# An attention and expert block on one core: expert products and two sides of a convolution issued behind the attention product, and k copied out of its bank ahead of q

## What is computed

```python
def window_attend(xh):                       # xh: 32 of the 64 channels
    q, k, v = split(einsum('oi,bihw->bohw', qkv_w, xh), 3)
    lepe = conv3x3_depthwise(v, lepe_w)
    q, k, v, lepe = part(q), part(k), part(v), part(lepe)    # 4x4 windows, 8 heads
    attn = softmax(q * scale @ k^T + bias)
    return unpart(attn @ v + lepe)
...
for s in (0, 2):                             # plain, and rolled by 2 rows and columns
    results.append(concat([window_attend(half) for half in halves(roll(ln_c(x), -s))]))
x = x + results[0] + roll_back(results[1])
t = tokens(x)
p = softmax(ln_t(t) @ router_w + router_b); top 2 of 8, renormalised
t = t + sum_over_top2(p * (ln_t(t) @ expert_w[e] + expert_b[e]))
```

## Time and profile before

| what | value |
|---|---|
| median of 3 runs | 3418.93 us (3413.72 to 3419.05) |
| the profiled execution | 3416.38 us, span 3414.6 us |
| mean granted TensorE clock | 0.942 of full |
| PE busy | 3076.2 us (90%) |
| POOL busy | 2509.8 us (74%) |
| DVE busy | 2233.1 us (65%) |
| ACT busy | 1619.7 us (47%) |
| DMA engines | mean share of some 60%, 152 GB/s |

### The profile page before, as it was taken

The page is one execution under the profiler, slowest core; times in us unless marked ns, Lnnn a source line. Parts: engine busy times, 40 slices in busy tenths (PEclk is TensorE's granted clock), DMA queues, the critical chain, the costliest instruction groups (busy, mean ns, idle before and its releaser), DMA issues.

```text
span 3414.6 us, 201082 instructions
## 1 busy us (share of the span) xinstructions
PE 3076.2 (90%) x84772; PEld 1798.8 (53%) x84772; DVE 2233.1 (65%) x4807; ACT 1619.7 (47%) x3362; POOL 2509.8 (74%) x4998
## 2 busy tenths in 40 slices
PE   4899999989989899998999989999899999999987
PEld 2555555545555455554555545555455555555553
DVE  2566767656666666666666757666666666666666
ACT  2554545445444454444444445444454444444441
POOL 4887777767777677777777767777677777777771
PEclk7999999999999999999999999999999999999998
DMA  2456665656565565556565656666565656565656
GB/s 64 105 138 160 159 160 155 160 131 168 148 167 149 145 165 147 155 153 153 150 168 147 163 139 158 161 155 166 133 170 148 168 152 163 152 162 146 163 138 178
DMA packets 436964, 517.64 MB, mean 152 GB/s; under 512 B 116400, under 2 KB 405168, under 8 KB 435888
## 3 DMA queue, kind: packets, MB, share of 16 engines
q1 hardware_dynamic: 270128, 390.67, 42.8%
q0 software_dynamic: 165888, 113.57, 13.9%
HBM read 312.67 MB, written 77.86 MB: 114 GB/s over the span
## 4 chain that ended last, share of the span: by engine, by line
PE 81%; issue 8%; DVE 5%; ACT 4%; DMA 1%; DVEq 0%; POOL 0%; SPq 0%; ACTq 0%; POOLq 0%
PE bank L632 18%; PE bank L717 14%; PE bank L697 13%; PE bank L617 9%; PE bank L723 4%; PE bank L657 3%; PE bank L670 3%; PE bank L737 3%; PE bank L742 2%; PE bank L731 2%; PE bank L756 2%; PE bank L648 2%; PE bank L748 2%; ACT qx L820 2%; ACT bank L812 1%
## 5 line engine op out<-in xcount | busy, mean ns | idle before, releaser
L585 POOL DMA_DIRECT2D vx<-vt x3072 | 1562.1, 517 | 443.6 <-PE bank L723 433.8
L573 POOL DMA_DIRECT2D kx<-k_sb x1536 | 739.2, 489 | 386.7 <-issue 241.7
L717 PEld LDWEIGHTS bank<-probT,vx 128*32 128x32 f32 x36864 | 605.5, 150 | 445.9 <-issue 387.8
L717 PE MATMUL bank<-probT,vx 128*32 128x16 f32 x36864 | 668.0, 210 | 146.9 <-issue 132.7
L632 PEld LDWEIGHTS bank<-kx,qx 32*32 32x32 f32 x36864 | 598.1, 112 | 345.4 <-issue 332.4
L632 PE MATMUL bank<-kx,qx 32*32 32x64 f32 x36864 | 700.7, 226 | 76.6 <-issue 54.2
L949 DVE TENSOR_TENSOR gx<-gate_wide,yn_pair 128x768 f32<-128x768 f32 x384 | 365.6, 953 | 384.5 <-PE bank L617 380.4
L697 PE MATMUL bank<-halo,conv_w 128*64 128x380 f32 (+6 forms) x2592 | 479.5, 497 | 0.1
L806 ACT ACTIVATE prob<-prob 128x512 f32<-128x512 f32 x576 | 360.0, 625 | 244.4 <-DVE prob L961 222.3
L961 DVE TENSOR_TENSOR prob<-bank,row_max 128x512 f32<-128x512 f32 x576 | 398.5, 692 | 16.7
L956 DVE TENSOR_REDUCE row_max<-bank 128x32 f32<-128x512 f32 x576 | 382.8, 665 | 37.8 <-PE bank L632 33.2
(11 more groups left out here) (72 smaller groups left out, 2959.9 us busy)
## 6 DMA issues: line engine op xcount, KB each, us to landing
gate_wide<-gate_rows SPq DMA_DIRECT2D x768, 192.0 KB, 3.9
vx<-vt POOLq DMA_DIRECT2D x3072, 12.0 KB
halo<-xn SPq DMA_DIRECT2D x160, 240.0 KB
kx<-k_sb POOLq DMA_DIRECT2D x1536, 24.0 KB
z<-fin SPq DMA_DIRECT2D x192, 192.0 KB
yn_pair<-yn POOLq DMA_DIRECT2D x384, 96.0 KB, 3.2
xa<-in_x SPq DMA_DIRECT2D x96, 192.0 KB, 3.1
xn<-xa SPq DMA_DIRECT2D x192, 96.0 KB, 2.5
```

Of the source, the lines that this page charges most:

```text
L573: pool.dma_start(kx[to + m:to + C:4, r % 2, m, :], k_sb[at + m:at + C:4, r % 2, :])\
L585: pool.dma_start(vx[to:to + TOK, r % 2, col:col + 25:8, odd, :], vt[at:at + TOK, r % 2, x::2, :, :].rearrange("p h n k -> p h (n k)"))\
L717: last = MM(bank_o[32 * c:32 * c + 32, at * TOK:(at + 1) * TOK], vx[:, kr % 2, :, at % 2, at // 2 * 4 + ba], probT[:, kr % 2, at, ba * TOK ...
```

## The change

Three things move, nothing is added or taken away. On TensorE sides 1 and 2 of the convolution (slots 5 and 0), expert 2 (slot 1) and expert 3 (slot 2) are issued behind the product of their slot; expert 3 gets the key (2, 1) for that. The router and centre still follow the sides. On ScalarE k is copied ahead of the two copies of q. On VectorE y_out moves from the middle of slot 2 to its end.

```diff
-EXPERT_AT = {(0, 0): 0, (1, 0): 1, (1, 1): 2, (2, 0): 3}
+EXPERT_AT = {(0, 0): 0, (1, 0): 1, (1, 1): 2, (2, 1): 3}
...
+                def conv(sides):
+                    ti = s.in_tile("conv")
+                    if not ti or ti[2] not in sides:
+                        return
                     k, r, side = ti
                     t, dw = (r + 1) % IMT, SIDES[side]
                     if side == 0:
...
                     if side == 2:
                         last.then_inc(conv_made, 1)
+
...
-                expert(1)
...
-                if (ti := s.in_tile("conv")) and ti[2] < len(SIDES):
...
+                conv((0,))
                 if u := s.unit("product"):
                     n, r = u
                     k, kr, j = s.in_strip("product")
...
                     last.then_inc(pv_made, 1)
+                expert(1)
+                conv((1, 2))
                 if ti := s.tile("centre"):
...
                 if st := s.strip("query_key"):
+
+                    k, r = st
+                    act.wait_ge(k_made, k + 1)
+                    if s.later(r, 2):
+                        act.wait_ge(k_spread[r % 2], k // 2 * (K_DMAS * 16))
+                    S.activation(by_window(k_sb[:, r % 2, :]), windows(bank_p[1][:, 0:SPX]),
+                                 ACT.Copy).then_inc(k_saved, 1)
+                if st := s.strip("query_key"):
                     k, r = st
                     if s.later(r, 2):
                         act.wait_ge(score_made, (k - 1) * UNITS)
...
-                if st := s.strip("query_key"):
-
-                    k, r = st
-                    act.wait_ge(k_made, k + 1)
-                    if s.later(r, 2):
-                        act.wait_ge(k_spread[r % 2], k // 2 * (K_DMAS * 16))
-                    S.activation(by_window(k_sb[:, r % 2, :]), windows(bank_p[1][:, 0:SPX]),
-                                 ACT.Copy).then_inc(k_saved, 1)
...
                 gate_product(0)
-                if yt := s.tile("tile_out"):
-                    k, r = yt
-                    dve.wait_ge(expert_made, (k + 1) * PAIRS)
-                    if s.later(r, 2):
-                        dve.wait_ge(out_stored[r % 2], k // 2 * 16)
-                    V.tensor_tensor(y_out[:, r % 2, :], bank_f[:, 0:SPX], y[:, r % 4, :], ALU.add).then_inc(y_out_made, 1)
...
                 gate_work((10, 12), (0, 0))
+                if yt := s.tile("tile_out"):
+                    k, r = yt
+                    dve.wait_ge(expert_made, (k + 1) * PAIRS)
+                    if s.later(r, 2):
+                        dve.wait_ge(out_stored[r % 2], k // 2 * 16)
+                    V.tensor_tensor(y_out[:, r % 2, :], bank_f[:, 0:SPX], y[:, r % 4, :], ALU.add).then_inc(y_out_made, 1)
```

More of the change, by code:

```diff
@@ L619, in expert @@
                     last.then_inc(expert_made, 1)
+                def conv(sides):
+                    ti = s.in_tile("conv")
+                    if not ti or ti[2] not in sides:
+                        return
+                    k, r, side = ti
+                    t, dw = (r + 1) % IMT, SIDES[side]
+                    if side == 0:
+                        pe.wait_ge(halo_loaded[r % 2], halos_to(s, r) * 16)
+                        if s.later(r, 1):
+                            pe.wait_ge(y_step, k * 2 - 1)
+                    low, high = max(0, -dw), W - max(0, dw)
+                    first = [side == 0, side == 0]
+                    for group, skip in ((0, 0), (1, 2)):
+                        parts = [(half, *rows) for half in range(2) for rows in conv_rows(t, half)[group]]
+                        for half, top, end, which in sorted(parts, key=lambda part: part[1]):
+                            at = half * SP + skip
+                            last = MM(by_rows(bank_c[half * C:(half + 1) * C, 0:SPX])[:, top:end, low:high],
+                                      conv_w[:, which, group * 3 + side, :],
+                                      by_rows(halo[:, r % 2, :])[:, at + top:at + end, low + dw:high + dw],
+                                      start=first[half], stop=(side == 2 and group == 1), skip_group_check=True)
+                            first[half] = False
+                    if side == 2:
+                        last.then_inc(conv_made, 1)
                 if u := s.unit("score"):
```

## The result

The changed kernel takes 3320.29 us (median of 4 runs, 3301.59 to 3324.2) against 3416.32 us for the kernel before (4 runs, 3407.16 to 3419.05) beside it: ratio 0.972, 95% interval 0.9691 to 0.975, 96 us less. The profiled execution took 3319.92 us with a span of 3318.1, 96.5 us less than the span before.

The account below looks back on a forecast made before the run. TensorE, busy 90% of the span, was taken to bound the kernel with its waits and lowered clock. Terms -32 - 5 + 25 - 53 + 9 = -56 us took 3418.9 to 3363 us, range 3300 to 3420.

Parts of the forecast that it names:

- k ahead of q: Slot 3: k copied 0.92 us earlier on ScalarE shortens tile_sum's wait for k; -32 us, bounds 0 and -47.
- Bias: Score of slot 3: its wait for the bias goes in some 33 tiles; -5 us, bounds 0 and -18.
- Clock: TensorE behind slot 3's standstill: clock falls less often, 31 stretches of 1.71 us fewer; -53 us, at most 164.
- as about half the tiles keep gaps of near 2 us in sum: Step in sizing the clock gain: the reason to take only a third of the possible 164 us, giving -53 us.
- rival of the clock staying up: No standstill above 1 us in slot 3, so 137 us of clock return: sum -140, 3279 us; chance 0.13.
- 116 stretches: Low-clock stretches of TensorE over the span before the change, 198 us lost in all, more than one to a tile.
- Code blocks: Code-load gaps in slots 2 to 4 and 0: -35, +45 and +15 at most; together +25 us, bounds -35 and +60.
- 3.87 us from restart to restart: TensorE, product of slot 3 to score of slot 4: time between restarts after code gaps, taken to stay.
- The product of slot 5: Without side 1 as cover it waits 0.1 to 0.2 us for fin of the strip before; +9 us.
- Code loading takes it all back: Rival: loads of slots 2 to 4 set the pace, k's gain reappears as gaps; about -15 us, 3404; chance 0.17.
- Code loading doesn't care for the order: Rival: a gap is as long wherever the block ends, code term nought; sum -81, 3338 us; chance 0.08.
- Slower, by loads 2 us later: Rival: SP's loads, 2 us later, fall on the code load slot 4 waits for; 3440 us; chance 0.12.

Follow-up runs that it names:

- e4: The changed kernel with side 1 alone put back ahead of the product of slot 5, side 2 left behind that of slot 0: 3292.23 us, ratio 0.9682.
- e3: The changed kernel with all three sides of the convolution ahead of the product again; experts, y_out and k stay moved: 3280.94 us, ratio 0.965.
- e1: The kernel before with one edit, k alone copied ahead of q: 3370.12 us, ratio 0.9915 to the kernel before.
- e10: The kernel before with only experts 2 and 3 behind the product and y_out at the slot's end: 3360.97 us, ratio 0.989.
- e8: The changed kernel with gate rows spread over 16 of 384 columns, so part of the computation is left out: 3196.75 us, ratio 0.9401.

## Why the prediction came out as it did

The direction was right, and so was the mechanism: the shorter standstill of slot 3, worth more through the clock than through the wait. 3363 us was forecast, 3320 measured, and the sum of -56 us stands against -96. That the time still lies inside 3300 to 3420 is in part luck: the clock gave 62 us more than forecast and the terms against it took some 23 us more. The range's lower end left out the bound of the clock term that the prediction itself states (164 us could go, 111 more than forecast, which gives 3252). By its terms, on the two profiled spans:

- *k ahead of q*, -32 forecast: -31.7 (46.9 to 15.2). Right, 0.62 us being left in an unhindered tile for the 0.7 forecast. The 16 waits of 1.5 us and more (about 20 were counted) are gone.
- *Bias*, -5: -6.5.
- *Clock*, -53: **-115. This is the term that was mis-sized.** The step that failed is "as about half the tiles keep gaps of near 2 us in sum". 7 of the 74 tiles of the loop kept 1.6 us or more in slot 3 and the next score, where 66 had it before. The clock fell in 5 places in slots 3 and 4 for 56, and in 13 for 63 in all slots of the loop, where 31 stretches fewer were forecast in the whole program. Two short standstills in place of a long one are not the reason: only 6 tiles have such a pair. The rival of the clock staying up had 137 us here and was the nearer; its condition, no standstill above 1 us in slot 3, held in 57 of the 74 tiles (before, in 4). The 116 stretches, "more than one to a tile", came from dividing 198 us by the 1.71 of one tile; the trace has 87 falls before and 24 after, and 12 of the 87, some 43 us, lie in the first 150 us and behind 3250.
- *Code blocks*, +25, and here two of its parts failed. The gaps in the product of slot 3 shrank by 58 us (111.4 to 53.2) for the 35 forecast. Those in the score of slot 4 grew by 5 us (4.9 to 9.9) for the 45: only 13 tiles have a gap there, so the 3.87 us from restart to restart was no rule for the others. Slot 0 gained 20 us of gaps (37.2 to 57.5) for 15 at most, and slots 5 and 2, which the sum didn't have, 24 and 14 us.
- *The product of slot 5*, +9: the new wait for fin is there but small (4.4 to 6.0 us in the list). Its cover was priced against fin alone; without side 1 in that place the slot became 0.77 us a tile longer, 74 us if in all 96 tiles. 0.32 of the 0.77 is printed standstill, 0.06 clock, the rest is printed nowhere. Putting side 1 back took 0.53 us a tile off that slot (e4), both sides back 24 us off the kernel (e3).
- Together the last two had +34 us, against the +57 us that is left of the span, -96.5 + 31.7 + 6.5 + 115. The waits listed don't show it ("issue" even fell by 6 us); the lengths of the slots show where it lies, three quarters of the growth in slot 5 and a quarter in slot 0.
- *Code loading takes it all back*: not so. e1 and e10 show what was behind that rival: k alone gives a quarter and the experts alone a third of what they give together.
- *Code loading doesn't care for the order*: not so; gaps moved with the order in every kernel. The rival's "against" was not quite right either: 37.2 us of the 199.1 lay in slot 0, mostly in 9 gaps of 2.5 to 3.9 us at the start of a turn of the loop (the first at 748.66), which no kernel here removed. The section "Instruction fetch mechanics" of the Trainium skill's page "Runtime: NRT & Kernel Launch" has a block boundary as mostly hidden. The trace doesn't agree with the page here: the gaps come to 193.1 us in the changed kernel, and to 111.5 with less traffic (e8).
- *Slower, by loads 2 us later*: not so. Clock 0.975 was outside the 0.95 to 0.965 that was to be seen, on the good side; the k wait of 15.2 us just missed "under 15".

What stays open: 0.64 us a tile that is in no printed gap and in no low clock (modelled ends of matmuls may hide it, which no run separates), why the load of slot 5 begins later, whether side 2's new place matters at all (e4 doesn't resolve it), and what y_out, expert 2 and expert 3 did each by itself.

## What to carry to other kernels

Where an engine's clock follows its activity, price a standstill by what it does to the clock, and take that from a count of the tiles and not from one of them: here 115 us of clock came with 38 us of waits. Waits that cover each other (a copy and a code gap) must be removed together, as neither alone gives much. Before moving long matmuls away from small ones, ask what they cover; order the copies out of a bank by who waits for them in that slot, not once for all.

## What the runs showed of the hardware

- TensorE's granted clock followed its standstills: with 1.89 us of standstill a tile in slot 3 it fell from 2.4 to 1.2 GHz in 56 places in 74 tiles, with 1.42 to 1.72 us in 31 to 48, with 0.83 us and less in at most 6 (the table above).
- The "issue" gaps of TensorE are code loads: 244 of 245 end 1.1 to 2.1 us behind the end of a 16 KB transfer of the instruction queue, which takes some 1.2 us itself.
- They depend on the data traffic: with 374.44 MB in place of 517.64 MB moved and the same instructions they fell from 193.1 to 111.5 us. The time from one restart to the next was 3.87 and 3.89 us in two tiles in slots 3 to 4 and 5.85 us in slots 4 to 5, where the DMA share read 1.06.
- Useless work can leave the time as it is: two idle matmuls a tile put into a standstill raised the median clock from 0.946 to 0.953 at a ratio of 1.0016.
